# Scatters that wait for the zeroing of the ranges they reach, chunks of consecutive edges, and input loaded ahead of the zeroing

## The reference

```python
feat_in  = h @ W_in + b_in;  feat_out = h @ W_out + b_out
a_in  = segment_sum(feat_in[src]  * iw[:, None], dst)     # iw = edge_weight
a_out = segment_sum(feat_out[dst] * ow[:, None], src)     # ow = edge_weight_n2
...
msg = x[src] + edge_attr @ We[l].T + be[l]                # edge_attr is [50000, 64]
agg = segment_sum(msg, dst) * inv_deg
x = relu(agg @ Wl[l].T + bl[l] + x @ Wr[l].T)
```

## Time and profile before

| | |
|---|---|
| runs | 3142.1 us median of 3 (3141.87 to 3146.7) |
| the profiled execution | 3144.16 us, its span 3142.4 us |
| mean granted clock of TensorE | 0.95 of 2.4 GHz |
| busy share of the span | PE 83%, DVE 54%, ACT 40%, POOL 26% |
| moved by DMA | 440.30 MB, of them 149.35 MB in the first 389 us |

### The profile page before, as it was taken

How to read it: one execution, slowest core, us unless ns; L and a number is a source line. 1 busy time by engine, 2 the same in 40 slices (tenths; PEclk the granted TensorE clock), 3 DMA queues, 4 the chain that set the end, 5 groups by cost and what they waited for, 6 DMA issues and landing times.

```text
span 3142.4 us, 38353 instructions
## 1 busy us (share of the span) xinstructions
PE 2610.5 (83%) x15375; PEld 1439.8 (46%) x15375; DVE 1687.8 (54%) x1866; ACT 1264.6 (40%) x2580; POOL 822.5 (26%) x634
## 2 busy tenths in 40 slices
PE   0563888888888849899899799999999989899896
PEld 0421444444444425444444444565556655555543
DVE  4547999999999955555555453111122252223314
ACT  0113777777777736666666322011011121212203
POOL 3000078888887762222222000000000000000000
PEclk9776999999999979999999899999999999999897
DMA  9999822222222237777776533322322223332341
GB/s 372 402 381 402 344 19 18 15 19 18 19 15 19 15 70 260 243 238 236 233 241 209 147 74 107 109 78 98 107 84 92 85 87 128 109 115 95 96 147 61
DMA packets 210271, 440.30 MB, mean 140 GB/s; under 512 B 84427, under 2 KB 128700, under 8 KB 209862
## 3 DMA queue, kind: packets, MB, share of 16 engines
q1 hardware_dynamic: 134764, 408.55, 38.5%
q0 software_dynamic: 60768, 18.76, 6.8%
q10 hardware_dynamic: 14553, 10.47, 1.1%
HBM read 287.68 MB, written 150.02 MB: 139 GB/s over the span
## 4 chain that ended last, share of the span: by engine, by line
PE 49%; SPq 11%; POOL 11%; DVE 10%; DMA 7%; issue 6%; ACT 4%; DVEq 0%; ACTq 0%; POOLq 0%
PE psum L1079 25%; POOL cell_mat L535 11%; SPq L370 11%; PE psum L1027 11%; PE psum L959 6%; DVE AR L1405 4%; DMA cell_mat<-ROW 4%; ACT Q L673 3%; DVE Q L1450 2%; PE psum L973 2%; DMA Q<-cell_mat 1%; PE psum L1096 1%; ACT Q L664 1%; DMA cell_mat<-SA 1%; PE psum L1106 1%
## 5 line engine op out<-in xcount | busy, mean ns | idle before, releaser
L1079 PE MATMUL psum<-FR 125*128 125x500 f16 (+1 forms) x4200 | 822.7, 354 | 20.8 <-DVE FR L1504 20.8
L1405 DVE TENSOR_SCALAR AR<-Q,ROW 128x3125 f16<-128x3125 f16 x391 | 722.6, 1903 | 9.0 <-PE psum L916 1.8
L911 PE MATMUL psum<-AR,Q 128*128 128x500 f16 x2346 | 571.6, 379 | 138.9 <-DVE AR L1405 122.4
L535 POOL DMA_INDIRECT cell_mat<-ROW x391 | 617.2, 1578 | 159.6 <-issue 106.4
L1079 PEld LDWEIGHTS psum<-FR 125*128 125x128 f16 x4200 | 387.4, 98 | 429.5 <-issue 44.8
L1531 DVE SCALAR_TENSOR_TENSOR Q<-psum,small,ROW 128x1000 f32<-128x1000 f32 (+1 forms) x42 | 48.2, 1148 | 713.2 <-PE psum L1079 713.1
L911 PEld LDWEIGHTS psum<-AR,Q 128*128 128x128 f16 x2346 | 199.1, 98 | 361.7 <-DVE AR L1405 129.9
L1450 DVE SCALAR_TENSOR_TENSOR Q<-Q,small 125x1000 f16<-125x1000 f32 (+1 forms) x175 | 252.4, 1446 | 205.4 <-ACT Q L673 204.8
L1027 PE MATMUL psum<-wl,Q 128*125 128x256 f32 (+1 forms) x1100 | 286.8, 401 | 5.7 <-ACT Q L730 3.0
L673 ACT ACTIVATE Q<-Q,small 125x1000 f16<-125x1000 f32 (+1 forms) x175 | 262.0, 1497 | 60.7 <-DMA Q<-cell_mat 60.5
L973 PE MATMUL psum<-Q,FR 125*128 125x500 f16 (+1 forms) x1050 | 237.8, 365 | 55.9 <-DVE Q L1450 54.3
(11 more groups left out here) (291 smaller groups left out, 2757.8 us busy)
## 6 DMA issues: line engine op xcount, KB each, us to landing
cell_mat<-SA SPq DMA_DIRECT2D x39, 3000.0 KB, 32.3
Q<-cell_mat SPq DMA_DIRECT2D x150, 750.0 KB, 5.3
FR<-count_mat SPq DMA_DIRECT2D x180, 625.0 KB, 3.8
count_mat<-Q SPq DMA_DIRECT2D x150, 125.0 KB, 4.9
FR<-in_edge_attr POOLq DMA_DIRECT2D x13, 960.0 KB, 9.4
Q<-in_edge_attr SPq DMA_DIRECT2D x41, 256.0 KB, 2.7
cell_mat<-ROW POOLq DMA_INDIRECT x391
Q<-cell_mat SPq DMA_DIRECT2D x25, 187.5 KB, 2.8
```

The costliest lines, as they stand in the source:

```text
L535: pool.indirect_dma_start(out=cell_mat, out_offset=bass.IndirectOffsetOnAxis(ap=at[c % VALS][:, k:k + 1], axis=0), in_=vals[c % VALS][:, k ...
L911: pe.matmul(a, own_attr, onehot[t % 3][:, t0:t0 + nt], start=t == 0, stop=t == ET - 1, skip_group_check=True)
L1079: last = pe.matmul(a[:, hh, 0:w], parts[:, c, t, f], slot(m, j)[0:P, i_, :], start=t == 0 and c == 0, stop=t == NT - 1 and c == 1, skip_gr ...
L1405: dve.tensor_scalar(onehot[t % 3], iota16, dst_c[:, t:t + 1], None, ALU.is_equal).then_inc(S["onehot_ready"], 1)
```

## The change

It has five pieces.

1. **Order of the edges.** Chunk c now holds the consecutive edges 1024 c to 1024 c + 1023; edge `8 p + k` of a chunk is edge p of its tile k. The arrays are loaded as 48 rows of 1024 numbers, turned by 32 transposes on PE and copied to their places by DVE. The last 7 tiles are loaded as before. The chunks of attributes are read in the same order.
2. **Waits of the scatters.** The zeroing is counted by range (`zero_in`, `ranges_zeroed`). DVE finds the highest range that each of 7 parts of 56 tiles reaches (`reach`, `need`), PE turns that, and POOL reads the 7 numbers into registers and waits at the start of each part until so many ranges are zeroed.
3. **Input first.** SP waits until `x` and the weights of layer 1 are in (`x_in`, `raw_in`) before it writes zeros. It writes 38 slabs and one third of a slab instead of 39 slabs.
4. **Feature loop.** Eight buffers `hT` instead of four (now in tile `FR`), and ACT copies the transposed tile t before it takes the results of tile t-1.
5. **Peak loop.** The reductions over the features stand between those over the attributes (after loads 4, 6, 8, 10 and 12). Attribute chunks 2 to 13 are loaded through ACT's queue inside the edge loop.

```diff
@@ sync
+            for i, b in enumerate((src, dst, edge_w, edge_w2)):
+                rows_i = edge_ints[:, i * 128 * EC:(i + 1) * 128 * EC] if i < 2 else edge_rows[...]
+                sp.dma_start(rows_i, b[0:FULL * 128 * EC].rearrange("(c e) -> c e", c=FULL)).then_inc(S["edges_in"], 16)
...
             sp.wait_ge(S["zeros"], 1)
-            for j in range(3 * CELLS // SLAB):
-                sp.dma_start(flat_cells[j * SLAB:(j + 1) * SLAB]..., zero_block...).then_inc(S["zeroed"], 16)
+            sp.wait_ge(S["x_in"], 32)
+            sp.wait_ge(S["raw_in"], 16 * 4 * LAYERS)
+            sp.dma_start(flat_cells[3 * DUMP:3 * DUMP + 3 * 512]..., zero_block[0:2, 0:768]).then_inc(zero_in[0], 16)
+            slabs = [0] * NR
+            for j in range(3 * DUMP // SLAB + 1):
+                k = REPEAT if j < 3 * DUMP // SLAB else LAST_ZERO
+                g = min(r for r in range(NR) if j * SLAB < 3 * N * COLS * (r + 1) or r == NR - 1)
+                slabs[g] += 1
+                sp.dma_start(flat_cells[j * SLAB:j * SLAB + 128 * ZERO * k]..., zero_block...).then_inc(zero_in[g], 16)
+            for r in range(NR):
+                sp.wait_ge(zero_in[r], 16 * (slabs[r] + (r == 0)))
+                sp.sem_inc(S["ranges_zeroed"], 1)
@@ gpsimd
-            for c in range(EARLY):
-                if c >= 2:
-                    pool.wait_ge(S["attr_lo"], c - 1)
-                pool.dma_start(attr32[c % 2], attr_main[:, EC * c:EC * c + EC, :]).then_inc(early_in[c % 2], 16)
-            pool.wait_ge(S["zeroed"], 16 * (3 * CELLS // SLAB))
+            for c in range(2):
+                pool.dma_start(attr32[c], attr_chunk(c)).then_inc(early_in[c], 16)
+            pool.wait_ge(S["reach_ready"], 1)
+            ranges_needed = [pool.value_load(need[0:1, i:i + 1], min_val=1, max_val=NR) for i in range(REACH)]
             for t in range(ET):
                 c, k = divmod(t, EC)
+                if t % RT == 0:
+                    pool.wait_ge(S["ranges_zeroed"], ranges_needed[t // RT])
@@ scalar
-            for t in range(NT):
-                act.wait_ge(S["tr_done"], TR_AT["feat", t])
-                if t >= 4:
-                    act.wait_ge(hT_out[t % 4], 16 * (t // 4))
+            for t in range(NT + 1):
+                if t < NT:
+                    act.wait_ge(S["tr_done"], TR_AT["feat", t])
+                    if t >= 8:
+                        act.wait_ge(hT_out[t % 8], 16 * (t // 8))
...
+                if k == 0 and c + 2 < EARLY:
+                    act.wait_ge(S["attr_lo"], c + 1)
+                    act.dma_start(attr32[c % 2], attr_chunk(c + 2)).then_inc(attr_in[c % 2], 16)
@@ tensor
+            pe.wait_ge(S["edges_in"], 16 * 12)
+            pe.wait_ge(S["edge_step"], 1)
+            for i in range(4):
+                for k in range(EC):
+                    last = pe.transpose(psum[:, i, k * FULL:(k + 1) * FULL], edge_rows...[:, i, :, k], ident[0:FULL, 0:FULL])
...
+            pe.wait_ge(S["reach_step"], 1)
+            pe.transpose(psum[0:1, 7, 0:REACH], reach_top, ident[0:REACH, 0:REACH]).then_inc(S["reach_step"], 1)
@@ vector
+            dve.tensor_copy(edge_rows[:, 0:2 * 128 * EC], edge_ints).then_inc(S["edge_step"], 1)
...
+            dve.wait_ge(S["edges_turned"], 1)
+            for i, v in enumerate((src_f, dst_c, w_e1, w_e2)):
+                last = dve.tensor_copy(tile_order(v), turned_edges(i))
...
+            for i in range(REACH):
+                last = dve.tensor_reduce(reach[:, i:i + 1], cell_less[:, i * RT:min((i + 1) * RT, ET)], AX.X, ALU.max)
...
+                if i in FEATURES_AFTER:
+                    feature_peaks(FEATURES_AFTER[i])
```

More of the change, by code:

```diff
@@ L63, in build_gnn @@
     PEAK_TILES = EM // PEAK_LOADS
-    EARLY = 7
+    EARLY = 14
+    FULL = EM // EC
+    REACH = 7
+    RT = -(-ET // REACH)
+    FEATURES_AFTER = {4: 0, 6: 1, 8: 2, 10: 3, 12: 4}
     IN_STEPS = [(r, t) for r in range(NR) for t in range(NT)]
@@ L290, in build_gnn @@
         S = {n: sem(n) for n in names}
-        hT_out = [sem(f"hT_out{s}") for s in range(4)]
+        hT_out = [sem(f"hT_out{s}") for s in range(8)]
         peak_in = [sem(f"peak_in{s}") for s in range(2)]
+        zero_in = [sem(f"zero_in{r}") for r in range(NR)]
         attr_in = [sem(f"attr_in{s}") for s in range(2)]
@@ L405, in load_epilogue @@
                 sp.dma_start(hT_now[r % 2][:, :, 0:nt * P], hT_d[:, :, t0 * P:(t0 + nt) * P].rearrange("h p n -> p h n")).then_inc(epi_in[r % 2], 16)
-            for s in range(4):
-                sp.wait_ge(hT_out[s], 16 * len(range(s, NT, 4)))
+            for s in range(8):
+                sp.wait_ge(hT_out[s], 16 * len(range(s, NT, 8)))
             for s in range(4):
@@ L592, in _ @@
                     act.wait_ge(S["peak_read"], PEAK_LOADS + 1)
+                    for s in range(8):
+                        act.wait_ge(hT_out[s], 16 * len(range(s, NT, 8)))
                 act.activation(feat[b][:, now, 0], Bn[b][:, now], ACT.Copy, scale=scale0[0:P, 0:1]).then_inc(S["feat_hi"], 1)
@@ L612, in attr_hi @@
             def attr_hi(c):
-                if c < EARLY:
-                    act.wait_ge(early_in[c % 2], 16 * (c // 2 + 1))
+                if c < 2:
+                    act.wait_ge(early_in[c], 16)
                 else:
-                    act.wait_ge(attr_in[c % 2], 16 * len(range(EARLY + (c - EARLY) % 2, c + 1, 2)) + (16 if c == CH - 1 else 0))
+                    act.wait_ge(attr_in[c % 2], 16 * (c // 2) + (16 if c == CH - 1 else 0))
                 if c >= 2:
@@ L811, in _ @@
             pe.wait_ge(S["masks"], 5)
+            pe.wait_ge(S["edges_in"], 16 * 12)
+            pe.wait_ge(S["edge_step"], 1)
+            for i in range(4):
+                for k in range(EC):
+                    last = pe.transpose(psum[:, i, k * FULL:(k + 1) * FULL], edge_rows.rearrange("c (i p k) -> c i p k", i=4, k=EC)[:, i, :, k], ident[0:FULL, 0:FULL])
+            last.then_inc(S["edges_turned"], 1)
             pe.wait_ge(S["cell_ready"], 1)
+            pe.transpose(psum[0:REACH, 7, 0:128], reach, ident[:, :])
             for b in range(4):
@@ L1267, in _ @@
             turned_cells, flat_pieces = psum[:, 0, :], pieces.rearrange("p c b n -> p c (b n)")
+            dve.tensor_reduce(reach_top, psum[0:REACH, 7, 0:128], AX.X, ALU.max).then_inc(S["reach_step"], 1)
             for s in blocks:
@@ L1302, in _ @@
             over = lambda v: v.unsqueeze(1).to_broadcast([P, NT, D])
+            dve.wait_ge(S["reach_step"], 2)
+            dve.tensor_scalar(need, psum[0:1, 7, 0:REACH], 1.0, None, ALU.add).then_inc(S["reach_ready"], 1)
             dve.wait_ge(S["out_done"], 1)
@@ L1321, in _, with feature_peaks @@
             dve.wait_ge(S["stat"], 3)
+            def feature_peaks(g):
+                dve.wait_ge(S["nat_ready"], NAT_AT["feat", (g + 1) * ROWS - 1])
+                dve.wait_ge(S["out_read"], (g + 1) * ROWS)
+                for b in range(2):
+                    v = Bn[b][:, g * ROWS:(g + 1) * ROWS]
+                    dve.tensor_reduce(peaks_f[:, 0, g, b:b + 1], v, AX.XY, ALU.max)
+                    dve.tensor_reduce(peaks_f[:, 1, g, b:b + 1], v, AX.XY, ALU.min)
             for i in range(PEAK_LOADS + 1):
```

58 lines of the change are left out of this document (31 added, 27 removed).

## The result

The changed kernel takes 3135.3 us (median of 14 runs, 3129.5 to 3140.9); the kernel before, on the same chips, takes 3144.7 us (median of 14, 3139.1 to 3146.8). The ratio is 0.9972 with a 95% interval of 0.9964 to 0.998. So the change brings 9 us, where 52 were forecast, and the time lies outside the forecast range.

The account below looks back on a forecast made before the run. DVE's one-hot stream was taken as the longer, with POOL's scatters meeting it late. Starting DVE 62 us earlier (38 + 24) gives 1097, scatters beside slabs add 10: 1107, gain 52, 3092, median 3090; range 3080 to 3102 (0.45).

Parts of the forecast that it names:

- POOL under the slabs: POOL's scatters beside the zeroing: first scatter at 287 us, 29 tiles by 400, last landed 1107, 10 later than DVE alone.
- C: Rival: the start does not come forward, only the 24 us of the peak loop are gained, 3118 us; chance 0.08.
- The start, -38: Up to the mean: with input loaded first, DVE's wait for the mean ends at 61 us instead of 99.1.
- All in: Start of the kernel: `x` and the weights of layer 1, 5.2 MB, loaded by 27 us, with issues and edges.
- The peak loop, -24: DVE's peak loop: feature reductions, 28.0 us behind the loop, fill its waits for loads; only the last group costs 4 net.
- DVE's stream at 255.5 and unchanged in length: DVE's edge loop starts at 255.5 us instead of 317.5 and runs 391 x 2.08 as before.
- Zeroing ends at 400: Slabs of zeros: start 22 us later, write 2 MB less, share engines with attribute chunks and scatters, end at 400 us.
- 3.88 per tile beside slabs, landing 7.5: POOL's scatters while slabs run: landing 3.6 + 3.9 = 7.5 us, two under way, 3.88 us per tile.
- 1.94 afterwards, last landed at 1107, 3090 us: After the zeroing: 362 scatters at 1.94 us take 702, last landed 1107, 52 us gained, median time 3090.
- Rival D: Slower: each tile's 128 targets lie near one destination and may lengthen landings; 3176 us at 4.1, 3235 at 4.40; chance 0.07.
- Rival B: Scatters crawl beside slabs: 6.7 us per tile gives 3113 us, 13 per tile 3128; chance 0.15.
- Rival A: DVE stays the bound, as scatters hardly suffer or beat 1.94: 3080 us, down to 3066; chance 0.22.

Follow-up runs that it names:

- the first experiment: Changed kernel with `ranges_zeroed` raised inside SP's slab loop, 6 slabs behind the issue, instead of behind the whole loop: 3094.9 us, ratio 0.9841 to the kernel before.
- the sixth experiment: Changed kernel with ranges told inside the slab loop, and the reductions over features put back behind the peak loop: 3108.0 us, ratio 0.9896 to the kernel before.
- the third: Kernel before with one piece alone, the reductions over the features inside the peak loop (four buffers `hT`): 3137.6 us against 3143.2, ratio 0.9979.
- three experiments: Ranges told inside the slab loop, plus: slabs held for `x` only, 3105.4 us; features behind the peak loop again, 3108.0 us; slabs at once, 3120.8 us.

## Why the prediction was wrong

**The step that failed** is the first of "POOL under the slabs": "Ranges are no limit: part 0 needs range 0, about 7 of 38 slabs, at (389 - 5) / 39 = 9.8 us each done near 96 us. The first scatter can go at 347.9 + 1 - 62 = 287." It asked when the zeros land, and not who says that they have landed and what that engine must do first. The diff in front of the prediction shows the loop over `NR` behind the loop over slabs. The wait was for SP's stream, and it was put at nothing: that an issue holds its engine entered no term, though the chain of the kernel before gives SPq 11% of the span, which the prediction read as "the zeroing", and one row of SP's timeline in that kernel has it whole:

```profile
4.98 362.67 SPq L370 DMA_DIRECT2D cell_mat<-SA  x39
```

SP was at its 39 issues for 363 us there too; it cost nothing, since all that stood behind them waited for the end of the zeroing anyway. The change put a signal there that was wanted earlier. In its place the runs show: SP issues until 383, the first scatter starts at 384.1 instead of 287, and 390 intervals of 1.94 behind it give a last start at 384 + 757 = 1141, plus what is lost beside the last slabs; 1145.7 was measured. With the signal raised inside the loop the first scatter starts at 288.8.

None of the rivals named this. C had the right mark, a start that doesn't come forward, but for DVE, whose start came.

Point by point, with the first experiment where the changed kernel can't show a step:

- *The start, -38*: -35.6, but not by the way that was worked out. "All in" was taken at 27 us from 292 GB/s and came at 43. The window over the first 43 us of the changed kernel (columns as above):

```profile
0.00:43.00 43.00, 5.12 (x38) 4.49 (x39) 22.02 (x64) 1.28 (x1) 26.97 (x47) 1.00 1.05 212
```

  The DMA engines were full (share 1.05) at 212 GB/s. ACT's queue moved its 6.07 MB in 74.1% of that time, 190 GB/s, and POOL's queue, with two loads of attributes that the prediction left out, took 17.6%. The mean then hung on the weights and not on DVE:

```profile
42.85 5.58 PE L865 MATMUL psum<-ident,AR 128*128 128x128 f32 x24 [6.18 <-DMA AR<-in_L_gnn_We]
...
52.47 11.06 PE L885 MATMUL psum<-Q,gate 125*125 125x256 f32 x50
```

  From the weights to the mean PE needs 9.6 us here and 9.3 in the earlier trace rows, so "weights as late as 45" would have moved the mean from the predicted 49 to 54; that they would change nothing was wrong. DVE had `reach_top` ready at 50.9, some 1.5 us before that start. That -35.6 came near -38 is luck in part: two limits lay close together.
- *The peak loop, -24*: held. The loop starts 35.4 earlier and the edge loop 57.3, so -22; by the first and the sixth experiment it is 24.0. The 8 us that four buffers `hT` would cost show in the third as 7.
- *DVE's stream at 255.5 and unchanged in length*: 260.2, and 1.902 a one-hot. The kernel that waits for all ranges has the same DVE code and starts it at 255.1, so some 5 us here may be spread between executions.
- *Zeroing ends at 400*: 399.7 in the changed kernel, with a start 16 us later than thought; what was taken for it was too much by that.
- *3.88 per tile beside slabs, landing 7.5*: 4.06 in the first experiment. The chain of the changed kernel, further on, has the landing itself:

```profile
384.08 7.35 DMA cell_mat<-ROW
391.43 0.27 issue
391.69 6.81 DMA cell_mat<-ROW
```

  The price taken from the attribute chunks was right within 5% of the period. By the rule of the Trainium skill that was weighed ("DMA: Bandwidth & Descriptors", section on queues, rings and completion order) the landing would have stayed near 3.8. The trace disagrees: 6.8 to 7.4 here and 7.0 to 8.6 in the first experiment (the third scatter starts at 297.38; less 0.27 of issue and the first's 288.84 that is 8.3), with 2.9 to 5.4 and mostly 3.4 to 4.4 alone. The working had a whole scatter wait for one packet, while from 290 to 400 us of the first experiment POOL's queue shows 3988 packets for 28 scatters, 9 on each engine. SP's queue shows 10051 packets in 91.3% of the 16 engines' time, 0.16 us each; one of them before each packet of a scatter would make 5.0 (an estimate), still too little. What else lengthens the landing stays open.
- *1.94 afterwards, last landed at 1107, 3090 us*: 1.93, 1107.6 and 3094.9 once the signal is early. The rate was right, but it is set mostly by POOL itself (1.55 us busy and 0.30 between, before 337 of the 391 scatters of the changed kernel) and not by landings, which end the idle time before 51. The match to 0.6 us is closer than the terms: the sum has 362 intervals where 361 are left, its terms give 1104 and not 1107, and what was measured for them comes to some 4 us more.
- *Rival D*, narrow targets: refuted, 1.937 per tile with consecutive edges in each tile. *Rival B*, crawl: refuted, 4.06 and not 6.7. *Rival A*, DVE stays the bound: not the case in the first experiment, but only by 8.5 us; it is the case as soon as DVE loses 16 us (three experiments).

Where the gain went: DVE's 57 us became idle time at its end. The two kernels with early signals against the two without show it: "input first" moves DVE's edge loop forward by 36 and 38 us (296.1 to 260.2 and to 257.8) and the slabs back by 36. With late signals, where the slabs' loop sets the first scatter, that makes the kernel 10 us slower; with early ones, where DVE's lead counts, 26 us faster.

**The version to keep** is that of the first experiment, 3094.9 us, faster than both kernels. The eight buffers and the attribute chunks on ACT's queue were not timed alone.

## What to carry to other kernels

When a change lets work start "as soon as X has landed", find the engine that says so and read what stands ahead of that line in its stream; here a loop of large transfers held its engine for 340 of the 356 us that the transfers took. Where two streams run side by side, a piece of work is worth what it moves on the later one, and the sign of an edit can turn when another edit changes which that is. A price for contention taken from the nearest transfers that wait for the same load came within 5% here.

## What was not expected of the hardware

- An issue of a 3.07 MB transfer on SP's queue takes 7.9 us of SP's time in the median (0.6 to 22.7), with about four of them under way. The first two of the loop took 0.6 us each.
- The same shows on ACT's queue. The two issues of `x` (25 rows of 1 KB in each partition) took 15.9 us together. The 25 stores of transposed tiles, 0.13 MB each, show what more transfers under way do, with slabs filling the engines both times. In the kernel before, where at most four were under way, an issue took 0.37 us and ACT waited 21.8 us for landings; in the changed kernel, with up to eight, an issue took 3.6 us in the median. So full engines alone don't hold an issue. The views of the two lines:

```profile
L573 ACTq DMA_DIRECT2D hT_d<-Q x25: 365/366/411, 149.2 to 263.8; - x25
L602 ACTq DMA_DIRECT2D hT_d<-FR x25: 373/3581/7957, 109.6 to 209.3; - x25
```

  The waits for landings went, but ACT's own feature loop stood 62.2 us behind its issues:

```profile
ACT AR L613 <- issue: 62.2, 16, 7.2
```

- Full DMA engines moved 212 GB/s in the first 43 us, where 8987 of 9690 packets were under 2 KB, and about 400 GB/s in the slices that zeros fill.
